# Score levels of an RWKV time mix built in pairs: one run of 64x64 products for two levels, two r/k sets, other orders on every engine

## The reference

```
def step(state, inp):
    rt, kt, vt, wt = inp
    kv = kt[..., :, None] * vt[..., None, :]
    out = jnp.einsum('bhk,bhkv->bhv', rt, state + u[None, :, :, None] * kv)
    return (state * wt[..., None] + kv, out)
```

## Time and profile before

| | |
|---|---|
| median of 3 runs (lowest, highest) | 2990.78 us (2988.10, 2991.21) |
| the profiled execution, span from first to last instruction | 2992.0 us; the record has no other time of it |
| busy PE, PEld | 93%, 74% |
| busy DVE, ACT, POOL | 79%, 46%, 43% |
| mean granted clock of TensorE | 0.981 of full speed |
| HBM traffic | 36.5 MB, 12 GB/s over the span |

### The profile page before, as it was taken

The page is one execution under the profiler, slowest core; times in us unless marked ns, Lnnn a source line. Parts: engine busy times, 40 slices in busy tenths (PEclk is TensorE's granted clock), DMA queues, the critical chain, the costliest instruction groups (busy, mean ns, idle before and its releaser), DMA issues.

```text
span 2992.0 us, 79123 instructions
## 1 busy us (share of the span) xinstructions
PE 2776.9 (93%) x32963; PEld 2213.3 (74%) x32963; DVE 2361.1 (79%) x5345; ACT 1382.2 (46%) x2771; POOL 1284.1 (43%) x1457
## 2 busy tenths in 40 slices
PE   5789999999999999999999999999999999999876
PEld 4567777777777777777777777777777777777654
DVE  5766888888888888888888888888888888888664
ACT  1344444544454455455445545545554444554331
POOL 3344444445444444444444444444444444444320
PEclk8899999999999999999999999999999999999998
DMA  4000000000000000000000000000000000000000
GB/s 149 14 5 9 12 12 5 9 13 12 12 12 12 5 9 12 12 12 12 12 6 12 9 12 12 12 12 9 9 9 12 12 12 12 5 9 12 9 8 7
DMA packets 36832, 41.52 MB, mean 14 GB/s; under 512 B 3272, under 2 KB 35200, under 8 KB 36480
## 3 DMA queue, kind: packets, MB, share of 16 engines
q1 hardware_dynamic: 35696, 36.32, 3.8%
q10 hardware_dynamic: 784, 0.16, 0.0%
HBM read 28.08 MB, written 8.39 MB: 12 GB/s over the span
## 4 chain that ended last, share of the span: by engine, by line
PE 61%; DVE 22%; ACT 8%; issue 5%; POOL 3%; ACTq 0%; DVEq 0%; DMA 0%; POOLq 0%
PE ps_all L1456 10%; PE ps_all L1268 10%; PE ps_all L1276 7%; PE ps_all L1470 6%; PE ps_all L1507 5%; PE ps_all L1489 5%; PE ps_all L1374 4%; DVE sxrk L1130 3%; DVE att L1136 2%; PE ps_all L1260 2%; DVE stats L1028 2%; ACT mixin L916 2%; DVE chan L1074 2%; PE ps_all L1400 1%; PE ps_all L1306 1%
## 5 line engine op out<-in xcount | busy, mean ns | idle before, releaser
L758 POOL TENSOR_TENSOR mixin<-mixin,hT_tm 128x512 f32<-128x512 f32 x320 | 390.4, 1230 | 356.3 <-DVE mixin L1095 356.0
L1456 PE MATMUL ps_all<-chan,cwk 128*128 128x256 f32 x1536 | 374.4, 390 | 8.3 <-DVE chan L1074 5.4
L1130 DVE TENSOR_TENSOR sxrk<-sxrk,dec 128x512 f32<-128x512 f32 x384 | 274.2, 714 | 96.5 <-PE ps_all L1374 93.4
L1470 PE MATMUL ps_all<-cwv,chan 128*128 128x256 f32 x1536 | 344.1, 381 | 0.0
L1456 PEld LDWEIGHTS ps_all<-chan,cwk 128*128 128x128 f32 x1536 | 283.0, 191 | 63.1 <-issue 20.3
L1470 PEld LDWEIGHTS ps_all<-cwv,chan 128*128 128x128 f32 x1536 | 290.7, 191 | 38.8 <-ACT chan L858 0.3
L738 POOL TENSOR_TENSOR rstd<-var,powc 128x2 f32<-128x2 f32 x224 | 188.3, 841 | 240.9 <-DVE var L1034 239.9
L1095 DVE SCALAR_TENSOR_TENSOR mixin<-ps_all,vcol,sxrk 128x256 f32<-128x256 f32 x640 | 270.1, 475 | 24.0 <-PE ps_all L1306 10.7
L1374 PEld LDWEIGHTS ps_all<-sxrk 64*64 64x64 f32 x10240 | 168.3, 129 | 135.0 <-issue 134.8
L777 POOL TENSOR_TENSOR lora<-S,dec 128x256 f32<-128x256 f32 x128 | 91.1, 711 | 351.4 <-DVE S L1145 350.8
L1374 PE MATMUL ps_all<-sxrk 64*64 64x32 f32 x10240 | 200.9, 216 | 41.3 <-DVE att L1136 38.1
(11 more groups left out here) (185 smaller groups left out, 6305.0 us busy)
## 6 DMA issues: line engine op xcount, KB each, us to landing
...
```

The lines of the kernel that those rows point to most:

```text
L758: pool.tensor_tensor(m, m, hT["tm", l][:, :, :, 1:P + 1].rearrange("p k c t -> p (k c) t"), ALU.add).then_inc(ev["mixed"][b], 1)
L1130: v.tensor_tensor(rko, rko, t, ALU.mult).then_inc(ev["rk_lev"][b], 1)
L1456: ins = pe.matmul(bank(b, "ck", lj, "k")[:, m * TT:(m + 1) * TT], cwk[:, l, k, n:n + P], k_in[:, k, :], start=(k == 0), stop=(k == KC - 1))
L1470: ins = pe.matmul(bank(b, "cv", l, "v")[:, c * D:(c + 1) * D], relu[t // 2][:, t % 2, c * P:(c + 1) * P], cwv[:, l, t, :], start=(t == 0), ...
```

## The change

Levels are taken in pairs n = 1, 2, 3 (levels 2n-1 and 2n). There are two sets of r and k per layer: the old place in `sxrk`, and the first two thirds of `mixin`. The stage list of a layer gets four new kinds in place of DVE's `lev`:

- `sc.n`: DVE multiplies one half of r and k by the decays of level 2n-1 and writes the result into the other set; ACT copies the halves that are not scaled (two instructions).
- `lev.n` on PE: after `sc.n` on both engines, the 16 products of level 2n-1 on the old set and the 16 of level 2n on the new one, with no wait between them. Weight columns are 62, 60, 56, 48 and 34 for levels 2 to 6. The two banks hold both levels side by side (`level_at`).
- `rs.n`: DVE multiplies by the decays of level 2n in place.
- `cp.0`, `cp.n`, `cq.n`: the masked copies of the diagonal, of level 2n-1 and of level 2n; the last gives the banks back. Each waits for the copy before it.

The number of products, of DVE multiplications and of masked copies is as before. ACT has six more instructions per layer and block. The mixed inputs v, r, k and g use other thirds of `mixin`, so `sc.1` also waits for `pv`. All four engines have new lists for period, head and tail, and there are no `warm` stages any more.

```diff
--- before.py
+++ after.py
-    PE: """4/4 gu.1.1; 1/2 lev.1; 0/1 yt; 3/3 cr cv; 0/1 wo; 1/2 pv lev.2; 4/4 ht.1; 1/2 lev.3; 2/1 turn.cm; 4/4 dn; 1/2
...
+    PE: """1/2 pv; 0/1 lev.3; 4/4 gu.1.0; 0/1 kt; 1/2 lev.1; 0/1 so ov; 3/3 ck.2; 4/4 gu.1.1; 0/1 yt; 3/3 cr cv; 0/1 wo; 1/2 pg;
...
-WARM = [(7, 6), (7, 9), (7, 6), (7, 1), (5, 4), (7, 6), (7, 6), (6, 2), (6, 1), (7, 2), (7, 9), (7, 13), (5, 2)]
+WARM = []
...
-        between = {1: ("pv", l), 3: ("pg", l)}
-        for j in range(1, LEVELS + 1):
-            s += [("lev", (l, j))] + ([between[j]] if j in between else [])
+        s += [("pv", l), ("sc", (l, 1))]
+        for n in range(1, LEVELS // 2 + 1):
+            s += [("lev", (l, n)), ("rs", (l, n))] + ([("pg", l)] if n == 1 else [])
+            s += [("sc", (l, n + 1))] if n < LEVELS // 2 else []
+            s += ([("cp", (l, 0))] if n == 1 else []) + [("cp", (l, n)), ("cq", (l, n))]
...
-    "decay_in": (["pw2"], 1), "decay": (["pw2"], 1), "gate_sig": (["pg"], 1), "ru": (["pr"], 1), "tots": (["tot"], 6), "diag": (["tot"], 1),
-    "rk_lev": (["lev"], 1), "khalf": (["kt"], 1),
-    "state_decayed": (["st"], 1),
+    "decay_in": (["pw2"], 1), "decay": (["pw2"], 1), "gate_sig": (["pg"], 1), "ru": (["pr"], 1), "tots": (["tot"], 6), 
+    "scaled": (["sc"], 1), "halves": (["sc"], 2), "rescaled": (["rs"], 1), "khalf": (["kt"], 1),
...
-            return mixin[b][:, (0, 1, 0, 2, 1)[f]]
+            return mixin[b][:, (0, 2, 0, 1, 2)[f]]
...
+        rk_sets = [(rk[b], mixin[b][:, 0:2]) for b in range(L)]
+        r_last, k_last = ([mixin[b][:, a] for b in range(L)] for a in range(2))
...
+        def level_at(j):
+            return {1: 0, 2: 3 * W // 4, 3: 0, 4: W // 4, 5: W // 2, 6: 3 * W // 4}[j]
...
+            def sc(i, b, ln):
+                l, n = ln
+                half = 1 << (2 * n - 2)
+                old, new = (rk_sets[b][(n + x) % 2] for x in (1, 0))
+                if n == 1:
+                    after(act, i, "ru", b, "pr", l)
+                    filled(act, i, b, "pv", l, "v")
+                else:
+                    after(act, i, "rescaled", b, "rs", (l, n - 1))
+                for a in range(2):
+                    to, of = (flat(x[:, a]).rearrange("p (m two h) -> p m two h", two=2, h=half)[:, :, a, :] for x in (new, old))
+                    act.activation(to, of, ACT.Copy).then_inc(ev["halves"][b], 1)
...
+            def scale(b, j, old, new):
+                t = decays(b, j).rearrange("p (n a) -> p a n", a=2)
+                to, of = (x.rearrange("p a k t -> p (a k t)")[:, half:2 * W - half].rearrange("p (a m) -> p a m", a=2) for x in (new, old))
+                if half == 1:
+                    to, of = to[:, :, 0::2], of[:, :, 0::2]
+                else:
+                    to, of = (x.rearrange("p a (m h) -> p a m h", h=half)[:, :, 0::2, :] for x in (to, of))
+                    t = t.unsqueeze(3).broadcast_to([P, 2, W // 2 // half, half])
+                return v.tensor_tensor(to, of, t, ALU.mult)
+            def sc(i, b, ln):
+                l, n = ln
+                if n == 1:
+                    after(v, i, "decay", b, "pw2", l)
+                    after(v, i, "ru", b, "pr", l)
+                    filled(v, i, b, "pv", l, "v")
+                else:
+                    after(v, i, "tots", b, "tot", l, 2 * n - 2)
+                    after(v, i, "rescaled", b, "rs", (l, n - 1))
+                scale(b, 2 * n - 1, rk_sets[b][(n + 1) % 2], rk_sets[b][n % 2]).then_inc(ev["scaled"][b], 1)
+            def rs(i, b, ln):
+                l, n = ln
+                after(v, i, "tots", b, "tot", l, 2 * n - 1)
+                filled(v, i, b, "lev", ln, "a")
+                scale(b, 2 * n, rk_sets[b][n % 2], rk_sets[b][n % 2]).then_inc(ev["rescaled"][b], 1)
...
+            def cp(i, b, ln):
+                l, n = ln
+                if not n:
+                    own = banks(b, "lev", (l, 1), "a")[:, :, 0:NC * KC * 3 * HH // 2].rearrange("p e (g m) -> p e g m", m=3 * HH // 2)[:, :, :, 0:HH]
+                    v.copy_predicated(att[b][:, :, :, :], dmask[:, :, :].unsqueeze(1).broadcast_to([P, HP, NC * KC, HH]), own).then_inc(ev["copied"][b], 1)
+                    return
+                if n == 1:
+                    after(v, i, "copied", b, "cp", (l, 0))
+                masked(b, ln, 2 * n - 1).then_inc(ev["copied"][b], 1)
+            def cq(i, b, ln):
+                l, n = ln
+                after(v, i, "copied", b, "cp", ln)
+                v.sem_inc(passed, 1)
+                masked(b, ln, 2 * n).then_inc(free_of(b, "lev", ln, "a"), 1)
...
-                v.tensor_tensor(rko, rko, t, ALU.mult).then_inc(ev["rk_lev"][b], 1)
-                v.copy_predicated(odd, mask, data).then_inc(free_of(b, "lev", lj, "a"), 1)
...
-            def lev(i, b, lj):
-                l, j = lj
-                half = 1 << (j - 1)
-                fill(pe, i, b, "lev", lj, "a")
-                if j == 1:
+            def lev(i, b, ln):
+                l, n = ln
+                fill(pe, i, b, "lev", ln, "a")
+                if n == 1:
                     after(pe, i, "ru", b, "pr", l)
+                after(pe, i, "halves", b, "sc", ln)
+                after(pe, i, "scaled", b, "sc", ln)
                 pe.sem_inc(pe_passed, 1)
+                for j in (2 * n - 1, 2 * n):
+                    half = 1 << (j - 1)
+                    r, k_ = (rk_sets[b][(n + j) % 2][:, x] for x in range(2))
+                    rows = max(HH - half, HH // 2 + 2)
+                    for c in range(NC):
+                        for k in range(KC):
+                            for e, q in TILES:
+                                p, t, g = slice(e * HS, (e + 1) * HS), slice(c * P + q * HH, c * P + (q + 1) * HH), c * KC + k
+                                a = bank(b, "lev", ln, "a", e)
+                                if j == 1:
+                                    ins = pe.matmul(a[q * HH:(q + 1) * HH, g * 3 * HH // 2:(g + 1) * 3 * HH // 2], k_[p, k, t],
+                                                    bonus[b][p, (k * NC + c) * 2 + q, :], start=True, stop=True)
+                                    continue
+                                at = level_at(j) + g * HH // 2
+                                odd = r[p, k, t].rearrange("p (n two h) -> p n two h", two=2, h=half)[:, :, 1, :]
+                                ins = pe.matmul(a[q * HH:q * HH + rows, at:at + HH // 2].rearrange("p (n h) -> p n h", h=half),
+                                                k_[p, k, t.start:t.start + rows], odd, start=True, stop=True)
+                ins.then_inc(full_of(b, "lev", ln, "a"), 1)
...
-                            rows = half if j == LEVELS else HH
-                            ins = pe.matmul(a[q * HH:q * HH + rows, g * HH // 2:(g + 1) * HH // 2].rearrange("p (n h) -> p n h", h=half),
-                                            kk[b][p, k, t.start:t.start + rows], odd, start=True, stop=True)
...
-                after(pe, i, "rk_lev", b, "lev", (l, LEVELS))
+                after(pe, i, "rescaled", b, "rs", (l, LEVELS // 2))
...
```

376 lines of the change are left out of this document (180 added, 196 removed), and 4 rows, old and new, of the table MIX_PSUM.

## The result

The changed kernel takes 3148.42 us (median of 4 runs, 3143.09 to 3153.07) against 2990.99 us (4 runs beside it): ratio 1.0528, 95% interval 1.0515 to 1.0541. Slower by 157 us where 43 us less were forecast. Of the rivals E held, in its direction; the time is beyond its 3039. The profiled execution of the changed kernel (span 3141.3 us) is the fastest of its four, so between the two profiles the difference is 149 us.

What follows compares the result with a forecast made beforehand. PE's own work was taken as the bound, 84.2 us of an 87.0 us period. 2992.0 - 48 (periods) - 3 (head and tail work) + 5 (clock) + 3 (quantisation), less 1.2, gives 2948 us, range 2925 to 2970.

Steps and rivals of the forecast that it cites:

- E: DVE, working its list in order, sets the pace; slower, 3039 us, if PE idles over 4.5 us a period; chance 0.12.
- What bounds it: Middle of the run: PE's own work, 84.2 us of each 87.0 us period, is the bound.
- I leave PE's idle time in a period at 2.8 us: Repeating period: new PE waits of 1.8 us offset by waits that go; idle stays 2.8 us, bounds 1.5 and 6.0.
- The wait at `turn.cm`: PE, stream 2: reaches `turn.cm` 17.5 us behind `ov`, its input comes at 18.8, so it waits 1.3 us.
- Fewer changes of shape: PE's list: 13 fewer tile shape changes a period at 0.10 us each gain 1.3 us, bounds nothing and 2.0.
- Columns: PE's levels: 28 fewer weight columns a layer and block gain 0.37 us a period, bounds +0.37 and -0.44.
- C: PE's levels: the tile, not columns, sets a weight load's price; 2971 us; chance 0.15 together with the clock.
- the prediction's own sign: Wrong outright if PE's busy time has not fallen by at least 1 us a period, or the head grows over 30 us.
- Sum: Whole kernel: 1.67 us gained a period over 28.7 periods makes 48 us; with head and tail terms, 2948 us.
- D: PE's levels: the 0.10 us is not the shape change, so only columns gain; 2985 us, no visible change; chance 0.06.
- Head +5 and +3: Head and tail: +5 us from the clock without identity products, +3 us from feed-forward weights' quantisation mostly ahead of first `wo`.
- ACT at nothing: ACT's six more copies a layer and block, 5.1 us a period, cost nothing; upper bound 1.7 us.

Runs made afterwards that it cites:

- the short GpSimd operations: Changed kernel with GpSimd's adds of mf and dn and product of yt cut from 512 columns to 8 or 16: 2979.54 us; same cut in kernel before: 2956.3 us.

## Why the prediction was wrong

- **What bounds it.** Right for the kernel before. The step that failed is "I leave PE's idle time in a period at 2.8 us", and under it "DVE has 417 / 500 x 87 = 72.5 us busy, so this is hidden": I read this as room, and moved DVE's operations with the durations that they had in their old neighbourhood. PE's idle time is 6.8 us, as DVE needs 80.0 us a period and not 72.6; without the collisions it is 3.1.
- **The wait at `turn.cm`**, foreseen at 1.3 us, is 32.5 / 22 = 1.5. That they are close is luck: the working used unslowed durations, and with these (the short GpSimd operations) the wait is 12.0 / 23 = 0.5.
- **Rival E** had the mechanism in outline, DVE setting the pace, and its limit (4.5 us idle) holds: 6.8. Its places were not right: no wait at `lev.3` among PE's largest, but `xt`, `mix` and `turn.cm`. What spoke for it, DVE busy 73 of 85 us, was understated (80.0 of 92.0), and what spoke against it, the steps counted up to `lev.3`, used the same unslowed durations. Its 0.12 was too small.
- **Fewer changes of shape, 1.3 us.** In a pair the second level starts 0.49 us behind the first at 64 columns, where a single one had 0.60; so 0.11 of the 0.60 belongs to the change too, and by these rows the upper bound (2.0) is nearer. By PE's busy time it is not: with the short GpSimd operations that falls from 83.9 to 83.1, and with 0.37 for columns and 0.7 lost (below) the changes are left with 0.8 - 0.37 + 0.7 = 1.1 us, near the 1.3. No run has this term alone.
- **Columns, 0.37 us.** Right: the levels of the kernel before with fewer columns save 0.013 + 0.026 + 0.054 + 0.107 - 0.013 = 0.19 us for a layer and block. Of the 11 us that 28.7 x 0.37 make, 5 were seen in the time of that run. C, the tile as price, is excluded by its 48 columns: 0.49 us, forecast 0.50, C 0.60.
- **A term not seen.** The 16 instructions of `mf` on PE (`mf.0` to `mf.3`), before and after, total of 46 runs from 500 to 2500 us (the second of the changed kernel with short GpSimd operations, to be free of collisions):

```profile
500.00:2500.00 2000.00, 55.87 (x736) 38.74 (x736) 1.00 0.04 11
```
```profile
500.00:2500.00 2000.00, 72.10 (x736) 48.94 (x736) 1.00 0.04 11
```

  16.2 / 46 = 0.35 us on average, 0.7 a period. In the stretch from 1500 to 1590 us it falls on one of the two layers: there the four instructions of `mf.2` now run behind the other twelve (2.02 us) and not between them (1.22). With it PE's busy time without collisions is 83.1 and not the forecast 82.5. In the changed kernel itself it is 85.2, above the 84.3 before: by the prediction's own sign, a busy time that has not fallen by 1 us a period, it was wrong outright. The falls of the clock can be part of this; it is not broken down.
- **Sum.** With the collisions away on both sides the period is 86.22 against 86.13: 0.8 us less PE work, 0.9 us more idle time (PE still waits at `mix`, `xt` and `turn.cm`, 13.8, 13.2 and 12.0 us in 2000). So the forecast gain of 48 us was gone even there. In the periods that is D's outcome, no change, for another reason than D's; the whole kernel would still be 23 us slower, most of it in the head.
- **Head +5 and +3.** 19 us, with and without collisions. Its cause stays open (above).
- **ACT at nothing.** Borne out: no wait of PE for the copies among its largest.
